# AdaLN-conditioned FFN: the first block's up product in two halves of 256 tokens, its weight squares, loads and expert products dealt out anew

## What is computed

```python
w = weights[conditions]                          # (128, 32, 32) of a table of 200
h = einsum('bct,bcd->bdt', x, w)                 # x: (128, 32, 256) -> 4096 tokens of 256
logits = h @ gate_w                              # 8 experts, the sum of the two largest is the scale
s = square(relu(h @ up_w)) @ down_w              # 256 -> 1024 -> 256
y = s + (h @ expert_weight) * scale
out = x + layernorm(y) * gamma + beta            # over the 256
```

## Time and profile before

| | |
|---|---|
| median of 3 runs | 233.61 us (233.34 to 233.93) |
| the profiled execution | 233.84 us, span of its instructions 232.1 us |
| PE | 222.0 us busy (96%) |
| PE weight load | 190.2 us (82%) |
| DVE | 149.4 us (64%) |
| POOL | 132.7 us (57%) |
| ACT | 106.6 us (46%) |
| DMA | 11.81 MB, mean 51 GB/s |

### The profile page before, as it was taken

How to read it: one execution, slowest core, us unless ns; L and a number is a source line. 1 busy time by engine, 2 the same in 40 slices (tenths; PEclk the granted TensorE clock), 3 DMA queues, 4 the chain that set the end, 5 groups by cost and what they waited for, 6 DMA issues and landing times.

```text
span 232.1 us, 3941 instructions
## 1 busy us (share of the span) xinstructions
PE 222.0 (96%) x1240; PEld 190.2 (82%) x1240; DVE 149.4 (64%) x377; ACT 106.6 (46%) x185; POOL 132.7 (57%) x129
## 2 busy tenths in 40 slices
PE   7798989999999999999999999999999999999991
PEld 2567878888888888888888888888888888888991
DVE  6457756666655666666666756656666666665885
ACT  2369853454454444444444544454445344444100
POOL 4635975477446564566554675456644675466522
PEclk9999999999999999999999999999999999999997
DMA  5692303120503002000200002000110002000111
GB/s 186 186 316 71 99 8 96 29 80 5 182 10 97 9 16 79 0 0 0 93 0 0 3 0 93 0 3 0 44 46 3 1 0 92 3 0 0 50 66 68
DMA packets 16889, 11.81 MB, mean 51 GB/s; under 512 B 6628, under 2 KB 16356, under 8 KB 16868
## 3 DMA queue, kind: packets, MB, share of 16 engines
q1 hardware_dynamic: 14084, 8.86, 12.7%
q10 hardware_dynamic: 2400, 2.65, 3.5%
q0 software_dynamic: 384, 0.05, 0.2%
HBM read 7.35 MB, written 4.19 MB: 50 GB/s over the span
## 4 chain that ended last, share of the span: by engine, by line
PE 84%; DMA 4%; issue 3%; DVE 3%; ACT 2%; ACTq 2%; POOLq 0%; POOL 0%; DVEq 0%
PE up_ps L257 33%; PE down_ps L317 25%; PE down_ps L319 13%; PE hid_ps L225 5%; DMA x_sb<-in_L_ffn_down_w_dram 4%; PE moe_ps L335 3%; PE moe_ps L333 3%; PE moe_ps L334 3%; ACTq L394 1%; ACT relu L371 1%; DVE square L428 1%; ACT L389 1%; ACT down_hl L383 1%; DVE hid_lo L420 0%; DVE down_hl L488 0%
## 5 line engine op out<-in xcount | busy, mean ns | idle before, releaser
L531 POOL TENSOR_TENSOR sq_lo<-square,sq_hi 128x512 fp32r<-128x512 f32 x64 | 83.0, 1299 | 65.4 <-DVE square L428 65.3
L317 PE MATMUL down_ps<-down_hl,sq_hi 128*128 128x512 f32 x248 | 88.7, 392 | 0.0
L319 PE MATMUL down_ps<-down_hl,sq_lo 128*128 128x256 f32 x248 | 69.6, 280 | 0.0
L428 DVE SCALAR_TENSOR_TENSOR square<-up_ps,relu 128x512 f32<-128x512 f32 x64 | 43.9, 688 | 36.1 <-ACT relu L371 36.1
L317 PEld LDWEIGHTS down_ps<-down_hl,sq_hi 128*128 128x128 f32 x248 | 46.5, 188 | 10.6
L371 ACT ACTIVATE relu<-up_ps 128x512 f32<-128x512 f32 x64 | 38.2, 596 | 33.1 <-PE up_ps L257 33.1
L257 PE MATMUL up_ps<-hid_hi,up_hi 128*128 128x512 f32 x128 | 51.9, 405 | 0.3 <-ACT hid_hi L358 0.3
L257 PE MATMUL up_ps<-hid_hi,up_lo 128*128 128x512 f32 x128 | 50.2, 392 | 0.0
L319 PEld LDWEIGHTS down_ps<-down_hl,sq_lo 128*128 128x128 f32 x248 | 46.7, 188 | 2.4
L373 ACT ACTIVATE sq_hi<-relu 128x512 fp32r<-128x512 f32 x64 | 40.5, 633 | 2.0
L257 PE MATMUL up_ps<-hid_lo,up_hi 128*128 128x512 f32 x128 | 40.1, 394 | 0.7 <-DVE hid_lo L420 0.7
(11 more groups left out here) (45 smaller groups left out, 201.3 us busy)
## 6 DMA issues: line engine op xcount, KB each, us to landing
x_sb<-in_x_dram SPq DMA_DIRECT2D x7, 512.0 KB, 3.5
out_dram<-result SPq DMA_DIRECT2D x7, 512.0 KB, 2.9
wd<-in_L_cond_weights_dram SPq DMA_DIRECT2D x110, 4.0 KB, 1.6
result<-in_L_ffn_up_w_dram ACTq DMA_DIRECT2D x2, 512.0 KB, 4.5
x_sb<-in_L_ffn_down_w_dram ACTq DMA_DIRECT2D x1, 1024.0 KB, 10.3
x_sb<-in_x_dram ACTq DMA_DIRECT2D x1, 512.0 KB, 3.4
out_dram<-result SPq DMA_DIRECT2D x4, 128.0 KB, 1.7
eg_raw<-L_ffn_expert_weight_dram SPq DMA_DIRECT2D x1, 256.0 KB, 3.5
```

The lines of the kernel that those rows point to most:

```text
L317: pe.matmul(dst[:, :], a_hi, down_hl[:, c, :, :].rearrange("p s t -> p (s t)"), start=(c == 0), stop=False)
L319: mm = pe.matmul(dst[:, T:2 * T], a_lo, down_hl[:, c, 0, :], start=False, stop=(c == CH - 1))
L428: dve.scalar_tensor_tensor(square[:, c % 2, :], up_ps[c % UPB][:, :], 0.0, relu[:, c % 2, :], ALU.max, ALU.mult).then_inc(square_done, 1)
L531: pool.tensor_tensor(sq_lo[:, j % 2, c, :], square[:, c % 2, :], sq_hi[:, j % 2, c, :].bitcast(f32), ALU.subtract).then_inc(sq_lo_done, 1)
```

## The change

- `conditioning_first(half)` does two groups at a time, into half banks: `hid_ps` and `moe_ps` for tokens 0 to 255, the two `down_ps` banks for 256 to 511. `hid_hi` and `hid_lo` of block 0 are made in four pieces of 256 (`hidden_first`).
- `first_chunks` does chunks 0 to 3 of block 0 in two halves of 256 tokens: the hi·hi and hi·lo products of chunks 0 to 2 for the first half, the conditioning of the second half, chunk 3, the lo·hi products of the first half, then the second half chunk by chunk.
- The first 16 squares go to SP, ACT and POOL in turn (6, 5 and 5).
- ACT's first activation, which brings the load of its table, stands ahead of its DMA issues.
- up is split in parts of 2, 2 and 4 chunks. `down_w` comes in two loads of 512 KB on SP's queue: ahead of x of block 1, and behind SP's squares of block 1. Parts 0 and 1 of down are split on ACT ahead of the first `rectify`, on DVE ahead of and behind the first `square_up`; parts 2 and 3 behind chunks 5 and 7.
- Experts of block 0's tiles 0, 1, 2 stand at c = 3, 5, 7 and tile 3 at c = 0 of block 1 (before: 1, 3, 5, 7).

```diff
-SPLIT_DOWN_AT = [(0, 1), (0, 3), (0, 4), (0, 6)]
-BY_SP, BY_POOL, BY_ACT = (0, 1, 2, 3, 8, 9), (4, 5, 6, 7), (10, 11, 12, 13, 14, 15)
+UP_SPLITS = [slice(0, 2), slice(2, 4), slice(4, CH)]
+DOWN_LOADS = 2
+FIRST = 4
+HALF_TOK = TOK // 2
+SPLIT_DOWN_AT = {5: 2, 7: 3}
+QUEUES = 3
...
+        def first_bank(half, k):
+            return ((hid_ps, moe_ps), down_ps)[half][k]
...
+        def experts_at(j, c):
+            if j == 0:
+                return {3: [(0, 0)], 5: [(0, 1)], 7: [(0, 2)]}.get(c, [])
+            if j == 1 and c == 0:
+                return [(0, 3)]
+            return [(j, c // 2)] if j < BLOCKS and c % 2 == 1 else []
...
+        def in_turn(queue):
+            return range(queue, TILES * Q, QUEUES)
...
             sp.dma_start(eg_raw[:, :, T:EG], gate_w.rearrange("(k p) e -> p k e", p=P)).then_inc(eg_landed, 16)
+            load_down(0)
             sp.dma_start(x_sb[:, groups(1), :], x_rows[:, groups(1), :]).then_inc(x_landed[1], 16)
...
+            load_down(1)
             sp.dma_start(beta_b[:, :], beta.rearrange("(o t) -> o t", o=1).to_broadcast([P, T])) \
...
+            def conditioning_first(half):
+                if half == 0:
+                    pe.wait_ge(x_landed[0], 16)
+                pe.wait_ge(wd_first_hw[half], count_hw(half))
+                pe.wait_ge(wd_first_pool[half], count_pool(half))
+                for k in range(K):
+                    condition(0, k, 2 * half)
+                    condition(0, k, 2 * half + 1).then_inc(hid_done, 1)
...
+            def first_chunks():
+                conditioning_first(0)
+                for c in range(FIRST - 1):
+                    first_rounded(c, 0)
+                conditioning_first(1)
+                first_rounded(FIRST - 1, 0)
+                for c in range(FIRST):
+                    first_rest(c, 0)
+                for c in range(FIRST):
+                    first_rounded(c, 1)
+                    first_rest(c, 1).then_inc(up_done, 1)
...
+            act.activation(table_loaded[:, :], nc.const_aps.tensor(0.0, [P, 1], f32), ACT.Copy)
             act.dma_start(x_sb[:, groups(0), :], x_rows[:, groups(0), :]).then_inc(x_landed[0], 16)
             act.dma_start(up_raw[:, :, up_cols(0)], up_rows[:, :, up_cols(0)]).then_inc(up_landed[0], 16)
-            act.wait_ge(consts_ready, 1)
-            act.activation(table_loaded[:, :], minus_half[:, :], ACT.Copy)
             act.wait_ge(cond_first_landed, 16)
...
             split_up(0)
-            act.dma_start(down_raw[:, :, :], down_w.rearrange("(c p) h -> p c h", p=P)).then_inc(down_landed, 16)
-            hidden(0, 0)
-            hidden(0, 1)
+            split_up(1)
+            for half in range(2):
+                for k in range(K):
+                    hidden_first(half, k)
+            split_up(2)
             act.wait_ge(eg_landed, 32)
             act.activation(eg_hi[:, :, :], eg_raw[:, :, :], ACT.Copy).then_inc(eg_hi_ready, 1)
-            split_up(1)
+            split_down(0)
+            split_down(1)
```

More of the change, by code:

```diff
@@ new lines, in up_ready, with first_rounded @@
+            def up_ready(c, ready):
+                for part, chunks in enumerate(UP_SPLITS):
+                    if c == chunks.start:
+                        pe.wait_ge(ready, part + 1)
+            def first_rounded(c, half):
+                if half == 0:
+                    up_ready(c, up_hi_ready)
+                if c == 0:
+                    pe.wait_ge(hid_hi_done, K * half + 1)
+                up_product(0, c, half_tok(half), up_hi, 0, hid_hi, 0)
+                if half == 0:
+                    up_ready(c, up_lo_ready)
+                up_product(0, c, half_tok(half), up_lo, 0, hid_hi, 1)
+                if c == 0:
+                    pe.wait_ge(hid_hi_done, K * half + 2)
+                up_product(0, c, half_tok(half), up_hi, 1, hid_hi, 2)
+                up_product(0, c, half_tok(half), up_lo, 1, hid_hi, 3)
@@ L297, in down @@
+                up_product(j, c, every, up_hi, 1, hid_lo, 5).then_inc(up_done, 1)
             def down(j, t, half):
@@ L348, in _ @@
                         down(j - 1, c // 2, c % 2)
-                    if j < BLOCKS and c % 2 == 1:
-                        experts(j, c // 2)
+                    for block, t in experts_at(j, c):
+                        experts(block, t)
                     if j + 1 < BLOCKS and c in round_at(j):
@@ L356, in hidden, with hidden_first @@
             def hidden(j, k):
-                act.wait_ge(hid_done, K * j + k + 1)
-                act.activation(hid_hi[:, j % 2, k, :], round_bank(j, k)[:, :], ACT.Copy).then_inc(hid_hi_done, 1)
+                act.wait_ge(hid_done, rounds(j, k))
+                act.activation(hid_hi[:, j % 2, k, :], hid_ps[:, :], ACT.Copy).then_inc(hid_hi_done, 1)
+            def hidden_first(half, k):
+                act.wait_ge(hid_done, K * half + k + 1)
+                act.activation(hid_hi[:, 0, k, half_tok(half)], first_bank(half, k)[:, 0:HALF_TOK], ACT.Copy) \
+                    .then_inc(hid_hi_done, 1)
             def scale_moe(j, t):
@@ L411, in _ @@
                     rectify(j, c)
-                    if (j, c) in SPLIT_DOWN_AT:
-                        split_down(SPLIT_DOWN_AT.index((j, c)))
+                    if j == 0 and c in SPLIT_DOWN_AT:
+                        split_down(SPLIT_DOWN_AT[c])
             scale_moe(BLOCKS - 1, TILES - 1)
@@ L507, in _ @@
                         square_up(j, c)
+                    if j == 0 and c == 0:
+                        split_down(1)
                     if j > 0 and c % 2 == 1:
@@ L511, in _ @@
                         total(j - 1, c // 2)
-                    if j < BLOCKS and c % 2 == 1:
-                        gate(j, c // 2)
+                    for block, t in experts_at(j, c):
+                        gate(block, t)
                     if j > 0 and c % 2 == 1:
```

162 lines of the change are left out of this document (83 added, 79 removed).

## The result

| | before | after |
|---|---|---|
| median | 233.77 us (233.34 to 235.26, 6 runs) | 231.92 us (231.81 to 232.02, 6 runs) |
| profiled execution, its span | 233.84, 232.1 | 231.90, 230.2 |

The ratio is 0.9928, 95% interval 0.9904 to 0.9951: faster by 1.9 us, where 3.2 was forecast. The time is inside the range, at 1.5 us above the forecast.

What follows compares the result with a forecast made beforehand. PE bounds the kernel, with idle time only at the start. Start -2.1, second conditioning +0.44, new idle +1.4, old idle -3.0 give -3.2 us, so 230.4 us, range 229.8 to 232.2.

Steps and rivals of the forecast that it cites:

- What bounds it: PE, busy 222.0 of 232.1 us; idle time lies ahead of 30.47 us, and a gain there reaches the end.
- the ruler: Start of tile 0's second half of down on PE, the same work ahead in both programs: 33.27 us before, 30.0 forecast.
- Halves cost nothing: In the first chunks, 48 matmuls of 256 columns take as long as 24 of 512; at worst 0.5 us more.
- Start: Conditioning begins at 7.3 us, released by SP's third square; first up matmul at 8.2, 2.1 us earlier.
- two matmuls: At the start, ACT copies 256 columns two matmuls after conditioning begins, at 7.7 us.
- Second half: Its conditioning stands inside the first chunks on PE and adds 4 x 0.11 = 0.44 us.
- land by 9.1: The second half's squares, last issued at 6.0 us, land by 9.1, ahead of PE's arrival at 9.65.
- Down: The first load of down, issued by SP at 7.3 us, lands at 12.8; PE no longer waits for it.
- Rival 1: Down's load lands late, ahead of every rectification: at 16.0 the gain is gone, at 17.6 it is 1.6 slower; 10%.
- Experts: PE waits 0.15 us ahead of chunk 4 and 0.9 at tile 1's experts, the gate standing behind square 3.
- The port: DVE's part 1 of down, at 15.1 us, goes ahead of POOL's first `sq_lo`, at 15.2; POOL waits 0.46.
- Rivals 3 and 4: DMA generally as slow as before, 231.6 to 232.0 (20%); table load holds ACT's DMA issues, 230.9 (5%).

Runs made afterwards that it cites:

- e5_no_halves: The changed kernel with chunks 0 to 3 of block 0 in whole 512-token matmuls behind both halves of the conditioning: 232.76 us (0.9991).
- e15_read8_warm12: `e14_in_turn_read8` with 12 matmuls on ones instead of 16: 231.90 us (0.9942).
- e7_table_behind: The changed kernel with the activation that brings ACT's table back behind the two DMA issues: 231.93 us (0.9940).
- e4_down_late: The changed kernel with the first load of down behind x of block 1 on SP's queue: 232.84 us (0.9974).
- e8_down_as_before: The changed kernel with down in one 1 MB load on ACT's queue, split behind chunks 1, 3, 4 and 6: 235.61 us (1.0093).
- e3_gate_early: The changed kernel with tile 0's gate behind square 1 and its scale on ACT ahead of rectification 3: 231.02 us (0.9896).
- e1_index16: The changed kernel, each queue reading all 16 indices of the first block in a row and picking its own: 232.21 us (0.9949).
- e11_up_split_and_gate: The changed kernel with tile 0's gate early and up's large part split between the halves of the hidden state: 230.96 us (0.9898).
- e14_in_turn_read8: `e11_up_split_and_gate` with the squares still in turn but their indices read 8 in a row for each half: 231.47 us (0.9916).

## Why the prediction was right in kind and too large

- **What bounds it, and the ruler: right.** The gain of 1.88 us at the ruler's point came out at the end, and PE is busy for all of 30 to 210 us. The profiled time lay 1.7 above the span, as before.
- **Halves cost nothing: nearly.** Neighbouring 256-column matmuls start 0.12 us apart in the timeline of PE, also behind another load. But 48 x 0.12 is 5.76 and 24 x 0.23 is 5.52, so the equation hid 0.2 us, and the chunks took 5.98 us in halves against 5.67 whole in `e5_no_halves`: 0.31, inside the stated bound of 0.5. What the halves bring is 0.8 us by that run, not the two us by which PE starts earlier.
- **Start: this step failed.** "POOL's two, at about 0.56 each, are early" left out what is ahead of them. Its read of the indices took 1.36 us instead of 0.52, and its second square landed at 7.8. That is 0.64 of the 0.99. The 16 matmuls on ones, until 7.45, would have been the next limit, and the sum had no term for them. The other 0.35 is between conditioning and the first up matmul: I counted "two matmuls" ahead of ACT's copy, but the profile lists four for two groups, as the earlier trace rows had listed two for one, and both the copy and what follows come later.
- **Second half: mis-sized for the same reason.** "4 x 0.11" counts one matmul for each group and round; the row at 10.83 has x8 and took 0.81. The ruler's own rounds, 8 x 0.11 for four groups, were right.
- **Its squares "land by 9.1": wrong, and it cost nothing here.** POOL's last took 3.9 us from 6.6, so 10.5, 0.3 ahead of PE's need at 10.8. Had PE been as early as forecast, it would have waited for them: at 9.65 by my sum. `e15_read8_warm12` shows just that, with 0.68 us of waiting, and in `e7_table_behind` a first up matmul 0.22 earlier left the ruler's point where it was. So even with the squares of the first half at 7.3, most of the missing 1 us would not have come; this is worked out from these two runs, and no run had both halves early.
- **Down: right.** Landed at 13.04 (12.8). Rival 1's mechanism held in `e4_down_late`: 1.5 us later, less 0.65 of slack, moved the relu by 0.85 and the median by 0.9. But what its move saves first is the squares beside it, by `e8_down_as_before`.
- **Experts: right, a little too dear.** The 0.15 us forecast ahead of chunk 4 did not come. The wait stood at tile 1, released by the moe, 0.64 for 0.9. The reason given (the gate stands behind square 3, which waits for `sq_lo` 1) is shown by `e3_gate_early`.
- **The port: right.** DVE was first. The Trainium skill, "SBUF — State Buffer", section "Who interferes with whom", lets the issue order decide who waits; the rows agree, 0.68 us where DVE was first (and 1.61 for POOL's `sq_lo` in place of 1.28) and 1.47 where POOL was, there with its addition of beta.
- **Rivals 3 and 4: no.** x of block 1 took 6.3 us and nothing waited for its squares; issues go on during the table load.

## What stays open

How long POOL's last square takes: issued at 6.6 behind the same loads, it landed after 3.9 us in the change, 4.4 in `e1_index16` and 4.5 in `e15_read8_warm12`, and I can't say why. And how much of the 0.5 us between `e11_up_split_and_gate` and `e14_in_turn_read8` is the later read, how much the length of the matmuls on ones, which was 5.0 to 6.4 us for the same 16. How often a wait of PE near 1.9 us at the second half's conditioning brings a lower clock is open too: one profiled execution shows it and one doesn't.

## What to carry to other kernels

An earlier start is worth no more than the latest of the things that reach PE at that place. Here the squares, behind the reads of their indices and beside large loads, landed at 7.8 and the 16 matmuls on ones ended at 7.45, and the next half's squares held PE again three microseconds later, so shorter reads or fewer matmuls on ones gave nothing by themselves. When work is dealt over queues anew, price what each queue does ahead of its first issue. And look on DVE for what stands behind a wait on another engine: a gate of 0.4 us moved two places ahead gave half as much as the whole change.
